# Expert weights laid out by partition in DRAM, and one load of the down weights per expert, in a two-layer audio tower kernel

## The reference, cut to what matters

```
# layer 0: 16 experts, 2 per token, capacity 320 slots, F = 352
x + _mlp(x, sw_gate, sw_up, sw_down) + output_tokens      # _mlp(h) = silu(h @ wg) * (h @ wu) @ wd
# layer 1: 64 experts, 3 per token, capacity 128 slots, H = 1024
h = gelu(einsum('ecd,edh->ech', buf, w1) + b1)
y = einsum('ech,ehd->ecd', h, w2) + b2
```

## Time and profile before

| | |
|---|---|
| runs of the kernel before (3) | median 1224.52 us, 1220.88 to 1227.47 us |
| the profiled execution | 1219.43 us, span 1217.7 us |
| mean granted TensorE clock | 0.957 |
| PE, PEld busy | 1093.2 us (90%), 895.7 us (74%) |
| DVE, ACT, POOL busy | 506.2, 518.1, 323.2 us |
| DMA | 218.95 MB in 153390 packets, mean 180 GB/s |

### The profile page before, as it was taken

How to read it: one execution, slowest core, us unless ns; L and a number is a source line. 1 busy time by engine, 2 the same in 40 slices (tenths; PEclk the granted TensorE clock), 3 DMA queues, 4 the chain that set the end, 5 groups by cost and what they waited for, 6 DMA issues and landing times.

```text
span 1217.7 us, 23672 instructions
## 1 busy us (share of the span) xinstructions
PE 1093.2 (90%) x7360; PEld 895.7 (74%) x7360; DVE 506.2 (42%) x2647; ACT 518.1 (43%) x1896; POOL 323.2 (27%) x319
## 2 busy tenths in 40 slices
PE   6999988688999999779889736999999999999996
PEld 5787776455666665457667626999999999999995
DVE  4689887421322322248888641222222222222221
ACT  1998888201111111079989702333333333333331
POOL 4144343301333344001424222222222222222222
PEclk9999998699999999989999857999999999999999
DMA  9623200005566663390100026999999999999990
GB/s 320 245 106 110 110 27 26 26 23 155 126 158 126 148 139 42 115 367 11 37 13 19 9 76 249 325 308 313 319 318 316 303 315 311 318 317 304 319 315 10
DMA packets 153390, 218.95 MB, mean 180 GB/s; under 512 B 15214, under 2 KB 125253, under 8 KB 152800
## 3 DMA queue, kind: packets, MB, share of 16 engines
q1 hardware_dynamic: 134368, 203.40, 48.9%
q0 software_dynamic: 18944, 14.62, 7.1%
HBM read 184.74 MB, written 43.09 MB: 187 GB/s over the span
## 4 chain that ended last, share of the span: by engine, by line
PE 62%; DVE 14%; issue 8%; DMA 7%; POOL 5%; ACT 4%; POOLq 0%; SPq 0%; DVEq 0%; ACTq 0%
PE bank L1111 19%; PE bank L1124 18%; PE bank L1051 5%; POOL rows L656 4%; PE bank L1008 4%; PE bank L1062 3%; DMA rows<-ffn_in,scatter_i 2%; DVE probs L1468 2%; ACT probs L1192 2%; PE bank L1018 2%; DMA early<-rows 2%; DMA stream<-arena,slot_token 2%; PE bank L799 1%; PE bank L778 1%; PE bank L1097 1%
## 5 line engine op out<-in xcount | busy, mean ns | idle before, releaser
L1369 ACT ACTIVATE dhidT<-bank,b1T 128x128 f32<-128x128 f32 x512 | 146.3, 369 | 308.3 <-PE bank L1111 308.2
L1111 PE MATMUL bank<-probsT,arena 128*128 128x128 f32 x2048 | 240.6, 276 | 0.0
L1111 PEld LDWEIGHTS bank<-probsT,arena 128*128 128x128 f32 x2048 | 235.1, 193 | 0.3 <-DVE probsT L1803 0.2
L1124 PE MATMUL bank<-arena,dhidT 128*128 128x256 f32 x1024 | 231.5, 379 | 0.0
L1124 PEld LDWEIGHTS bank<-arena,dhidT 128*128 128x128 f32 x1024 | 189.8, 190 | 23.2
L1192 ACT ACTIVATE probs<-probs,neg_max 128x128 f32<-128x128 f32 x512 | 197.8, 393 | 1.7 <-DVE neg_max L1468 1.4
L720 POOL DMA_INDIRECT out<-probsT,slot_token x64 | 98.6, 1541 | 375.5 <-DMA out<-probsT,slot_token 327.7
L1820 DVE TENSOR_TENSOR probsT<-bank,b_wide 128x256 f32<-128x256 f32 x64 | 27.2, 424 | 346.6 <-PE bank L1124 346.6
L656 POOL DMA_INDIRECT rows<-ffn_in,scatter_i x80 | 79.9, 998 | 206.3 <-DVE scatter_i L1608 176.7
L691 POOL DMA_INDIRECT stream<-arena,slot_token x48 | 72.5, 1511 | 172.0 <-DVE arena L1774 160.1
L1468 DVE CUSTOM_DVE_ANT_0 probs<-bank,mask 128x128 f32<-128x128 f32 x512 | 112.6, 283 | 11.2 <-PE bank L820 11.1
(11 more groups left out here) (162 smaller groups left out, 1333.6 us busy)
## 6 DMA issues: line engine op xcount, KB each, us to landing
arena<-L_ffn_w SPq DMA_DIRECT2D x128, 1024.0 KB, 7.2
rows<-zeros SPq DMA_DIRECT2D x13, 1024.0 KB, 8.3
drows<-rows SPq DMA_DIRECT2D x64, 132.0 KB, 7.4
arena<-L_ffn_w_gate SPq DMA_DIRECT2D x16, 352.0 KB, 3.8
arena<-L_ffn_w_up SPq DMA_DIRECT2D x16, 352.0 KB, 4.8
early<-rows SPq DMA_DIRECT2D x16, 264.0 KB, 2.7
early<-x SPq DMA_DIRECT2D x8, 512.0 KB, 4.5
arena<-L_ffn_w_down SPq DMA_DIRECT2D x16, 256.0 KB, 3.3
```

The source lines that it names most:

```text
L1111: mm = pe.matmul(bank[2 + 2 * (u % 2) + half][:, jj * P:(jj + 1) * P], w1_sb[u][:, c, j * P:(j + 1) * P], drowsT[:, u % 2, c, :], start=c ...
L1124: last_ = pe.matmul(bank[6 + u % 2][:, 0:D], dhidT[:, u % 2, j, :], w2_sb[u][:, j, :], start=j == 0, stop=j == J1 - 1)
L1369: last_ = act.activation(dhidT[:, u % 2, j, :], bank[2 + 2 * (u % 2) + half][:, jj * P:(jj + 1) * P], ACT.Gelu, bias=b1T[:, j, bass.ds(e, 1)])
```

## The change

Before the launch, `kernel()` lays each of the five arrays out anew: the rows are padded with zeros to whole chunks of 128 (only down's 352 rows need it, they become 384) and put in the order expert, partition, chunk, column. The views in the loads change so that partition p reads its chunks one after the other. `load_down` becomes one load, for all 128 partitions and three chunks, so its semaphore counts 16 per expert instead of 32. The matmuls still take only the 96 true rows of the last chunk. What is in `arena` is the same otherwise.

```diff
-    NE0, _, F0 = a["L0_ffn_w_gate"].shape
-    NE1, _, F1 = a["L1_ffn_w1"].shape
+    NE0, _, _, F0 = a["L0_ffn_w_gate"].shape
+    NE1, _, _, F1 = a["L1_ffn_w1"].shape
...
-                sp.dma_start(gate_w[u % 2], a["L0_ffn_w_gate"][bass.ds(e, 1)].rearrange("a (c p) f -> p (a c) f", c=DC)).then_inc(s, 16)
-                sp.dma_start(up_w[u % 2], a["L0_ffn_w_up"][bass.ds(e, 1)].rearrange("a (c p) f -> p (a c) f", c=DC)).then_inc(s, 16)
+                sp.dma_start(gate_w[u % 2], a["L0_ffn_w_gate"][bass.ds(e, 1)].rearrange("a p c f -> p (a c) f")).then_inc(s, 16)
+                sp.dma_start(up_w[u % 2], a["L0_ffn_w_up"][bass.ds(e, 1)].rearrange("a p c f -> p (a c) f")).then_inc(s, 16)
...
-                full = sum(m == P for _, m in FT)
-                sp.dma_start(down_w[u % 2][:, 0:full, :],
-                             a["L0_ffn_w_down"][bass.ds(e, 1), 0:full * P].rearrange("a (j p) d -> p (a j) d", p=P)).then_inc(s, 16)
-                sp.dma_start(down_w[u % 2][0:F0 - full * P, full:full + 1, :],
-                             a["L0_ffn_w_down"][bass.ds(e, 1), full * P:F0].rearrange("a p d -> p a d")).then_inc(s, 16)
+                sp.dma_start(down_w[u % 2], a["L0_ffn_w_down"][bass.ds(e, 1)].rearrange("a p j d -> p (a j) d")).then_inc(s, 16)
...
-                sp.dma_start(w1_sb[u], a["L1_ffn_w1"][bass.ds(e, 1)].rearrange("a (c p) f -> p (a c) f", c=DC)).then_inc(dw1_in[u], 16)
+                sp.dma_start(w1_sb[u], a["L1_ffn_w1"][bass.ds(e, 1)].rearrange("a p c f -> p (a c) f")).then_inc(dw1_in[u], 16)
...
-                sp.dma_start(w2_sb[u], a["L1_ffn_w2"][bass.ds(e, 1)].rearrange("a (j p) d -> p (a j) d", j=J1)).then_inc(dw2_in[u], 16)
+                sp.dma_start(w2_sb[u], a["L1_ffn_w2"][bass.ds(e, 1)].rearrange("a p j d -> p (a j) d")).then_inc(dw2_in[u], 16)
...
-                wait(pe, ed_in[u], 32 * (i + 1))
+                wait(pe, ed_in[u], 16 * (i + 1))
...
+    for name in ("L0_ffn_w_gate", "L0_ffn_w_up", "L0_ffn_w_down", "L1_ffn_w1", "L1_ffn_w2"):
+        experts, rows, cols = arrays[name].shape
+        chunks = -(-rows // P)
+        w = np.pad(arrays[name], ((0, 0), (0, chunks * P - rows), (0, 0))).reshape(experts, chunks, P, cols)
+        arrays[name] = np.ascontiguousarray(w.transpose(0, 2, 1, 3))
```

## The result

The changed kernel takes 1227.66 us in the median of 20 runs (1223.04 to 1232.85), the kernel before 1221.45 us in as many (1216.79 to 1227.87). The ratio is 1.0038, with a 95% interval of 1.0024 to 1.0052: slower by about 4.6 us (0.0038 of 1221.45; the two medians themselves are 6.2 us apart). The profiled execution took 1230.29 us, span 1228.6 us, which is 10.9 us over that of before; two single executions differ by more than the medians, and the traces are read with that in mind.

A forecast was written before the change was run, and what follows sets the result against it. PE was taken to bound layer 1's experts, with DMA close to full. The terms summed to -1 us: 1218.4 us against the profiled execution, 1223.5 us with the runs' median 5.1 us above it; range 1216 to 1230 us.

The forecast's parts named there:

- the sum (-1 us): All terms together: 0 everywhere except layer 0's rows landing sooner, 0.15 us x 7 = -1 us.
- Pieces of w1 and w2: Layer 1's expert weight loads: 65536 packets fewer, drain 5.0 instead of 5.3 us per expert, covered by PE's 7.25 us: 0.
- The adds of layer 1: POOL's adds in layer 1's experts: landing sooner as weight loads drain 0.3 us sooner, unseen by PE: 0.
- rival B: Layer 1's experts, 742 to 1200 us: DMA or the adds become the bound, +45 us, 1269 us; chance 0.08.
- First experts of layer 1: Loads of layer 1's first four experts, issued from about 512 us, far ahead of first use at 742 us: 0.
- the padding: Down's 32 rows of zeros in layer 0, 0.5 MB in all, some 0.09 us per expert, issued well ahead: 0.
- the wait for 16: PE waits for 16 instead of 32 on the semaphore of layer 0's down load: 0.
- SP loses one issue per expert: SP in layer 0's experts: 5.4 us of issues saved, covered by SP's own wait for slots: 0.
- every other expert it then waits for rows: Layer 0's experts: PE works 11.92 us per expert, then every other expert waits for rows; all such waits 13.5 us.
- +4 us: Layer 0's rows: larger bursts beside them could bring the median landing, 3.0 us, to the worst, 3.6 us.
- Rival A: Layer 0's experts: PE's waits for rows go, all 13.5 us of them, giving 1211 us; chance 0.10.
- Rival C: Loads still cut at the chunks; packets fall only by down's second load, 1224.5 us; chance 0.06.

The follow-up runs named there:

- cutting the chain there by other means: Kernel before with layer 0's slot tiles in four buffers instead of two, DVE's and POOL's loops written out: ratio 0.9896, 1212.18 us against 1223.82 us.
- the second group: Four kernels with 0.43 to 0.57 us between expert 4's row loads: changed (twice), down alone in one load, before plus one small load between; ratios 1.0025 to 1.0038.
- the first group: Six kernels with 0.04 to 0.06 us between expert 4's two row loads, among them the kernel before and the layout with down in two loads; ratios 0.9985 to 1.0005.
- its second measurement: Kernel before with ten empty instructions on SP between expert 4's row loads, which left no trace, so it counts as the kernel before again: ratio 0.9985.

## Why the prediction was wrong, point by point

The forecast was no measurable difference, and the time came out slower by 0.38%. The range in us held the median, but by luck: it allowed for rows that land at their worst because of larger bursts, and the runs with the old pieces show the same late landing. (Its upper end adds up to 1231 us rather than 1230; nothing hangs on it.) The sign of the sum (-1 us) was wrong and the difference is clear of its interval.

Pieces of w1 and w2: right. 65536 packets fewer from layer 1 and 60896 left in the queue, as worked out. The rate of 8 KB pieces was taken as 418 GB/s; slices of 418 and 434 show it. The 382 GB/s for the pieces of 1 KB was read from one slice; the next, 948 to 949, moves 413, so the gain of 0.3 us in the drain was, if anything, smaller. PE's 7.25 us per expert covered it, and layer 1's layout alone gives 0.9996.

The adds of layer 1: right. They land no later (6.2 us in the median against 6.3, over 47 adds each), and POOL's wait for them fell, though not its idle time in all. The lines are those of POOL's adds from 850 to 1190 us before, then from 860 to 1200 us in the changed kernel:

```profile
DMA to landing us min/median/max: 3.5/6.3/8.0
```

```profile
DMA to landing us min/median/max: 3.3/6.2/7.4
```

The Trainium skill (DMA: Bandwidth & Descriptors, section Queues, rings and completion order) says that an engine serves a whole packet before it goes to another queue. That an add would wait longer for its turn beside larger pieces did not show as a longer landing; rival B did not come.

First experts of layer 1, the padding, the wait for 16: no cost was found.

The step that failed is this one: "SP loses one issue per expert, 16 x 0.34 = 5.4 us. SP then waits for slots anyway [...], so the cover is SP's own wait: 0." The cover was named correctly for the time that the issue takes. But a removed instruction also moves what comes after it in SP's program, and SP's program has one place where it stands still for 0.44 us. The row was there: 299.38 + 0.37 = 299.75 us, and the next issue at 300.18 us. I had read only the distance of a later pair of loads of down (the row at 387.56 in the earlier trace rows), and did not look for irregular gaps on SP. I had also read the chain too kindly: "every other expert it then waits for rows" holds from expert 9 on, but from expert 4 to expert 9 PE waits for rows at every turn (0.47 to 0.98 us) in the trace of before. So the rows had no slack at all where the gap came to lie.

The second half of the same failure is the price of a wait. I priced a wait of PE at its own length, "+4 us" at the worst landing. The clock makes it longer: behind 1.8 us of waiting a product of 6.66 us took 8.35 us, at a granted clock of 0.79. The chain of before shows such a product, behind a wait of 2.7 us, and I took no row of it:

```profile
286.96 8.35 PE bank L1051 x24
```

With it the place costs 2.9 us where the longer wait alone is 1.2.

Rival A (the waits for rows go) did not come with the change: its place was right, and cutting the chain there by other means gives 1%. Its price of up to 13.5 us lies near the 11.6 us between the medians, but in part by accident: in the traces the wait of 2.8 us at the third turn stays, and from the turn of expert 3 to that of expert 15 it takes 8.2 us less (142.05 instead of 150.26). Rival C is excluded by the packets. What no rival had is a loss in layer 0's row path, though I named it as the only thing that could reach the path.

The signs I gave beforehand: the share of the queue fell by 2.7 points (I said 3 to 5), DMA in layer 1's experts is at 0.86 (0.8 to 0.88), and PE's waits at L1033, 11.7 + 3.4 = 15.1 us, stayed in the range of 9 to 18. That sum did not betray the loss, because long waits in fewer places add up to the same as short ones in more; the granted clock of the stretch did.

## What to carry to other kernels

Making DMA pieces larger paid nothing here, where PE was busy all of the time; read that first, and then look for what else the edit moves. Taking an instruction away from a queue shifts everything behind it, and where a chain has no slack, as the rows here, a delay of 0.4 us at one place can cost several times its length: the load itself landed later by more than the delay, and a wait that got long enough was followed by matmuls at the lower clock. Here the chain was better cut than tuned: the buffers of the slots gave 1%, and with them the same change cost nothing that could be measured.

## What the runs showed of the hardware that I had not expected

SP stands still for 0.43 to 0.44 us after its 79th recorded instruction. It does so in 13 of the 14 traces (both kernels and twelve runs, on more than one chip), whether a load of down, of rows or one issued with slack follows; in the one with three more loads ahead the place falls where SP waits anyway. There is no wait and no other instruction of SP in it. The traces hold one more sign of it: the profile's instruction queue q14, 43 and 44 packets in the two pages, brings a packet of 8192 bytes 1.55 to 1.79 us after the end of the 79th instruction in twelve of the fourteen (at 301.46 us before, at 311.55 us in the changed kernel), and where the place moves, that packet moves with it. This would fit a boundary at which a further piece of SP's program is brought in, but no run tests it; its cause stays open.

The second load of rows also landed later whenever it was issued late: 3.3 to 3.7 us after issue in the four kernels of the second group, 2.5 to 3.0 us in the first. Two of the four have the old gate and up layout, and one has the old down loads too, so the layout isn't the reason. The packets in the traces tell what goes with it. The two loads of rows are 320 pieces of 1056 bytes, the second 64 of them. In the first group the last 64 follow the others closely, take 47 to 63 ns each, and the rows end 0.1 to 0.7 us after the first piece of the gate load starts; the slow start (some 220 ns a piece in the kernel before) falls on gate's pieces, for which nobody waits. In the second group the last 64 take 107 to 171 ns each, and the rows end 0.9 to 1.5 us after gate's first piece starts. So the gap of 0.4 us parts the second load from the stream of the first and lets it fall in with gate's. Why a piece takes so long there stays open.

TensorE's clock (granted share 1.0 is 2.4 GHz, 0.5 is 1.2 GHz) does not follow from the length of a wait alone. PE's waits for rows from the turn of expert 3 on, in these kernels: every one of 1.8 us and more was followed by a product of 8.4 us instead of 6.7; of those from 1.1 to 1.7 us some were (1.14, 1.18, 1.26 us) and some were not (1.24, 1.39, 1.70 us); none below 1.1 us was. So in these traces a longer wait made a slow product likelier and didn't decide it, and single traces of the same kernel differ in their later slow products (none in the trace of before, one in its second measurement).

The empty instructions (`sp.nop`) left no trace in either kernel that had them and shifted nothing: SP's gap stayed at the 79th instruction, and ten of them between two loads left these 0.06 us apart.
